# Image tiles in four quarter-row transfers; first rows of a group and stacking copies on ScalarE's queue

## What is computed

```python
def tok(x, channel_weights):                      # x: (128, 12, 224, 224)
    pooled = x.reshape(B, C, 14, 16, 14, 16).sum(axis=(3, 5))
    return jnp.einsum('bcij,ce->bije', pooled, channel_weights).reshape(B, 196, 192)
def attn(x, proj_w, proj_b):
    q, k = x[:, :64], x[:, 64:]
    a = softmax(jnp.einsum('bqc,bkc->bqk', q, k) * scale)
    out = jnp.einsum('bqk,bkc->bqc', a, k)
    out = jnp.transpose(out, (0, 2, 1)).reshape(B, -1, 192) @ proj_w.T + proj_b
    return jnp.concatenate([out, k], axis=1)
def ffn(x, ...):                                  # cw: two experts' weights of each token
    h = silu(einsum('td,eid->tei', x, w1)) * einsum('td,eid->tei', x, w3)
    return einsum('tei,edi,te->td', h, w2, cw) + shared(x)
h = tok(x); h = h + attn(layernorm(h)); h = h + ffn(layernorm(h))
```

## Time and profile before

| | us |
|---|---|
| median of 3 runs | 1790.35 |
| lowest, highest | 1789.66, 1797.8 |
| the profiled execution | 1794.41 |
| its span, first to last instruction | 1792.6 |

### The profile page before, as it was taken

One profiled execution on the slowest core, in us unless ns is written; L12 is line 12 of the kernel. 1 busy time (PEld: TensorE's weight loads), 2 busy tenths in 40 slices (PEclk: granted clock), 3 DMA queues, 4 the chain that ended last, 5 costly groups with the idle time before them and its releaser, 6 DMA issues. The chain is left out here.

```text
span 1792.6 us, 29976 instructions
## 1 busy us (share of the span) xinstructions
PE 1509.6 (84%) x9094; PEld 1184.0 (66%) x9094; DVE 1178.3 (66%) x2060; ACT 879.1 (49%) x2809; POOL 761.5 (42%) x761
## 2 busy tenths in 40 slices
PE   1721698999899988989899988999899988999997
PEld 1201575877668765877668765777668765887686
DVE  5856686687768666667768676677768666355511
ACT  2333655556545645547535655546545644335310
POOL 4327244633373234623464243633373233733431
PEclk9955799999999989999999999999999989999998
DMA  9897777778677777777777687768777775223320
GB/s 341 358 361 276 300 276 272 276 276 291 245 280 260 281 262 268 273 275 274 256 247 297 241 292 278 276 253 299 256 263 280 268 262 158 70 64 111 96 84 24
DMA packets 127672, 440.11 MB, mean 246 GB/s; under 512 B 14221, under 2 KB 80930, under 8 KB 105998
## 3 DMA queue, kind: packets, MB, share of 16 engines
q1 hardware_dynamic: 126390, 436.79, 67.6%
q10 hardware_dynamic: 1112, 1.30, 0.3%
HBM read 413.86 MB, written 20.07 MB: 242 GB/s over the span
## 5 line engine op out<-in xcount | busy, mean ns | idle before, releaser
L752 POOL TENSOR_TENSOR ffn<-ffn 128x384 f32<-128x384 f32 (+2 forms) x448 | 510.3, 1144 | 888.7 <-ACT ffn L913 810.2
L1509 PE MATMUL bank<-W2T,ffn 128*128 128x192 f32 (+1 forms) x3600 | 705.7, 333 | 10.2 <-ACT stage L890 5.0
L1509 PEld LDWEIGHTS bank<-W2T,ffn 128*128 128x128 f32 (+1 forms) x3600 | 604.9, 191 | 79.8 <-issue 16.5
L1266 DVE TENSOR_TENSOR ffn<-bank,ffn 128x384 f32<-128x384 f32 (+2 forms) x504 | 310.4, 617 | 349.3 <-PE bank L1353 151.8
L960 DVE TENSOR_REDUCE pooled<-xt 128x3 f32<-128x768 f32 (+2 forms) x375 | 447.8, 1195 | 18.5 <-DMA xt<-in_x 17.9
L913 ACT ACTIVATE ffn<-bank 128x384 f32<-128x384 f32 (+2 forms) x504 | 272.3, 542 | 370.3 <-PE bank L1524 141.3
L801 ACT ACTIVATE xt<-xt 128x256 f32<-128x256 f32 x809 | 329.7, 414 | 83.7 <-DMA xt<-in_x 76.1
L1524 PE MATMUL bank<-X2T,Wx 126*128 126x384 bf16 (+2 forms) x720 | 202.6, 355 | 46.7 <-DVE ffn L1266 31.9
L801 ACT ACTIVATION_READ_ACCUMULATOR xt<-xt 128x1 f32 x809 | 158.6, 196 | 0.0
L1353 PE MATMUL bank<-x0h,WT0h 128*128 128x512 f32 x288 | 130.5, 453 | 6.0 <-DVE ffn L1266 6.0
L1524 PEld LDWEIGHTS bank<-X2T,Wx 126*128 126x128 bf16 x720 | 58.2, 100 | 103.7 <-DVE ffn L1266 46.1
(11 more groups left out here) (234 smaller groups left out, 1786.1 us busy)
## 6 DMA issues: line engine op xcount, KB each, us to landing
xt<-in_x SPq DMA_DIRECT2D x168, 1792.0 KB, 8.2
ffn<-cw_rows SPq DMA_DIRECT2D x192, 256.0 KB, 6.8
ffn<-cw_rows SPq DMA_DIRECT2D x192, 192.0 KB, 8.8
out<-stage SPq DMA_DIRECT2D x192, 96.0 KB
ffn<-cw_rows SPq DMA_DIRECT2D x64, 224.0 KB, 7.1
h2q<-Msb SPq DMA_DIRECT2D x64, 54.0 KB
ffn<-in_L_ffn_w SPq DMA_DIRECT2D x2, 768.0 KB
attw<-in_L_ffn_w SPq DMA_DIRECT2D x1, 512.0 KB
```

The source lines that it names most:

```text
L752: nc.gpsimd.tensor_tensor(out=cwb[slot][:, 0:n], in0=silu[(g.par + step) % 2][:, 0:n], in1=cwb[slot][:, 0:n], op=ALU.mult).then_inc(scaled, 1)
L1266: v.tensor_tensor(out=h[step % HR][:, 0:n], in0=h_ps(g, step, 1)[:, 0:n], in1=(silu[p] if e == NE else cwb[(c * NE + e) % CW_RING])[:, 0:n ...
L1509: last = mm(o, h[step % HR][:, 128 * t:128 * t + m], W2T[:, e, :], start=(e == 0 and t % 2 == 0), stop=(e == NE), skip_group_check=True)
```

## The change

Each tile is read by four DMAs of a quarter of a row (128 partitions by 3584 bytes) one behind the other instead of by one; all four count on the tile's semaphore, and the sums wait for all four as before. The copies of `stack_mix` become the ACT items `mix` in steps 11 and 17, and rows 0 to 4 of the next group ACT items `row` in steps 61 and 62, each with the same DMAs, now on ACT's own queue. SP issues the rows from 5 on as before, and the tiles.

```diff
-MIX = {11: 0, 17: 1}
+AQ_PLAN[11].append(("mix", 0))
+AQ_PLAN[17].append(("mix", 1))
...
+AK_PLAN[61] = [("row", 0), ("row", 1)]
+AK_PLAN[62] = [("row", 2), ("row", 3), ("row", 4)]
...
+PIECES = 4
...
-        v = 16 * ((self.off * TILES + t) // SLOTS + 1)
+        v = 16 * PIECES * ((self.off * TILES + t) // SLOTS + 1)
...
+        def load_tile(eng, num, t, slot):
...
+            for p in range(PIECES):
+                at = slice(ROW // PIECES * p, ROW // PIECES * (p + 1))
+                eng.dma_start(xt[:, slot, at], xv[num, i, 128 * k:128 * k + 128, at]).then_inc(x_in[slot], 16)
...
-                if use == 0:
+                if use == CW_AHEAD:
                     sp.wait_ge(cw_out[0], g.at(16, 16))
...
-                if step >= 61 and left:
-                    for ahead in ((0, 1) if step == 61 else (2, 3, 4)):
-                        cw_load(g.plus(1), ahead)
-                elif step + CW_AHEAD < STEPS and g.off >= 0:
+                if step + CW_AHEAD < STEPS and g.off >= 0:
                     cw_load(g, step + CW_AHEAD)
...
-                    if step in MIX:
-                        stack_mix(g, MIX[step])
...
+                if kind == "mix":
+
+                    act.wait_ge(aux_act, g.at(BYACT[-1], BYACT[R[("M", 2 * i + 1)]]))
+                    for m in range(4):
+                        act.dma_start(Mst[:, 4 * i + m, :],
+                                      Msb[2 * CH * m:2 * CH * (m + 1), i, :]).then_inc(mixed[i], 16)
+                    return
+                if kind == "row":
+
+                    if i == 0:
+                        act.wait_ge(cw_out[0], g.at(16, 16))
+                    back = i + CW_USES - CW_RING
+                    wait(act, h_done, g.minus(1).at(STEPS, back // NE * EX + back % NE + 1) if g.k is not None or g.off else 0)
+                    if i == CW_RING - 1 or g.k is None and g.off == 0:
+                        act.wait_ge(rows_used, POOL_TILES)
+                    n = CHUNKS[0][2]
+                    act.dma_start(cwb[i][:, 0:n], cw_rows[g.par, i, 1024:1024 + n].partition_broadcast(128))\
+                       .then_inc(cw_landed[i], 16)
+                    return
```

More of the change, by code:

```diff
@@ L236, in landed @@
     def landed(self, t):
-        v = 16 * ((self.off * TILES + t) // SLOTS + 1)
-        return v if self.k is None else self.k * (16 * 2 * TILES // SLOTS) + v
+        v = 16 * PIECES * ((self.off * TILES + t) // SLOTS + 1)
+        return v if self.k is None else self.k * (16 * PIECES * 2 * TILES // SLOTS) + v
     def bank(self, r):
@@ L410, in build @@
         xv = x.rearrange("(g b) c (s i h) w -> g i (b c s) (h w)", b=GB, s=2, h=PATCH)
-        def x_rows(num, t):
+        def load_tile(eng, num, t, slot):
             k, i = t // HALF, t % HALF
-            return xv[num, i, 128 * k:128 * k + 128, :]
+            for p in range(PIECES):
+                at = slice(ROW // PIECES * p, ROW // PIECES * (p + 1))
+                eng.dma_start(xt[:, slot, at], xv[num, i, 128 * k:128 * k + 128, at]).then_inc(x_in[slot], 16)
         PREP = [("CWcT", 0), ("CWcT", 1), ("G", 0), ("gate", 0), ("repG", 0), ("gate", 1)]
@@ L487, in _ @@
             for t in range(SLOTS):
-                sp.dma_start(xt[:, t, :], x_rows(0, t)).then_inc(x_in[t], 16)
+                load_tile(sp, 0, t, t)
             sp.wait_ge(cwr_ready, 1)
@@ L505, in load @@
                 slot = g.slot(t)
-                sp.dma_start(xt[:, slot, :], x_rows(g.num(), t)).then_inc(x_in[slot], 16)
+                load_tile(sp, g.num(), t, slot)
             def store(g, c):
@@ L526, in store @@
                     sp.dma_start(dst, st[0:min(n - 128 * t, 128), t, :]).then_inc(done, 16)
[L528 to L533, removed]
             def load_after(g, t):
@@ L556, in cw_load @@
                     sp.wait_ge(cw_out[2], g.at(32, 32))
-                if use in (0, NE, QCH * NE):
+                if use in (CW_AHEAD, NE, QCH * NE):
                     sp.sem_inc(sp_passed, 1)
```

## The result

| | median us | lowest, highest | runs |
|---|---|---|---|
| before, beside it | 1793.44 | 1783.66, 1800.71 | 20 |
| after | 1803.14 | 1790.14, 1815.14 | 20 |
| ratio after/before | 1.0053 | 95%: 1.0033 to 1.0074 | |

The changed kernel is 0.5% slower, 9.5 us by the ratio. Forecast was 1789 on a median before of 1790.35 us, so the middle of "no change"; the time lies inside the range of 1768 to 1808, but the kernel moved by more than its interval. The profiled execution of after took 1797.95 us, 5 us less than its median, and is only 3.5 us longer than that of before.

A forecast was written before the change was run, and what follows sets the result against it. PE sets the pace from group 0 on, DMA engines before it. Rows -9.9, quarters +6 and +1.5, copies removed -22.3, ACT's block +17.6 and +6 sum to -1.1 us: 1789 on a median of 1790.35, range 1768 to 1808.

The forecast's parts named there:

- Rows on ACT, -9.9: Rows 0 to 4 on ACT's queue: -10.2 us at six group boundaries, -1.7 for the clock, +2 ahead of group 0.
- 3.9 + 1.5 us: Row 0's landing time after ACT's issue: 3.9 us from a small `CQ` write, 1.5 for sharing with quarter tiles.
- the 1.7 us a boundary: At the boundary of two groups, row 0 issued by ACT would land near 591.5, 1.7 us earlier than before.
- rows come no earlier: Rival: rows on ACT interleave with the tiles, and each boundary loses up to 2.3 us; late half 1803 us; chance 0.12.
- Ahead of group 0, +2 and +6: Before group 0: ACT's five row issues delay its first silu, +2 us; eighteen quarter tiles while DMA-bound, +6 (0 to 9).
- The 11%: Packets of 3.5 KB would be 11% dearer than those of 14 KB, 0.5 us on a tile's 4.6 us.
- Later quarter tiles, +1.5 (0 to 5): From group 0 on, rows issued behind a tile come 1 us later for three more issues: +1.5 us (0 to 5).
- Copies removed at `H`, -22.3: PE's 12.0 us wait for stacking copies at the first `H` goes, with 10.3 us of lower clock after it: -22.3 us.
- ACT's block, +17.6 and +6 in step 11, 0 in step 17: Four copy issues delay ACT's silu behind the step 11 exp 2.2 us a group, +17.6; clock falls +6; step 17 free.
- Signs: POOL's row waits under 40 us, PE's L1402 under 5, L1449 none for copies; exp to silu 4.6; group 0 8 later.
- block and clock at double weight: Rival: clock falls at step 14 in most groups and issues don't run beside the exp: 1806 us, chance 0.18.
- The last rival: PE's waits were another's, so the change pays prices without gains: 1797 us; counted within the forecast's chance of 0.37.

The follow-up runs named there:

- quarters_only: Kernel before with only the image tiles split into four quarter-row transfers, rows and copies staying on SP: ratio 1.0083 to before, +14.9 us.
- quarters_rows: Kernel before with quarter tiles and rows 0 to 4 issued by ACT, stacking copies staying on SP: ratio 1.0076 to before, +13.6 us.
- before_wide: Kernel before with one edit, each query chunk's four two-image stores made eight one-image stores: 1761.09 us, ratio 0.9829 to before, -30.7 us.
- after_wide: Changed kernel (all three parts) with the query chunk's four two-image stores made eight one-image stores: ratio 1.0017 to before, +3.0 us.
- quarters_wide: Kernel before with one-image stores and quarter tiles, rows and copies staying on SP: ratio 0.9891 to before, -19.5 us.
- wide_mix1: Kernel before with one-image stores and only the stacking copies of step 17 issued by ACT: ratio 0.9881 to before, -21.3 us.
- mix_only: Kernel before with only the eight stacking copies of a group issued by ACT, tiles whole, rows on SP: ratio 1.0080 to before, +14.3 us.
- wide_mix: Kernel before with one-image stores and all stacking copies issued by ACT, tiles whole: ratio 0.9954 to before, -8.2 us.
- rows_mix: Changed kernel with image tiles whole again, rows 0 to 4 and stacking copies still issued by ACT: ratio 1.0218 to before, +39.1 us.
- wide_rows: Kernel before with one-image stores and rows 0 to 4 issued by ACT, tiles whole: ratio 0.9895 to before, -18.8 us.

## Why the prediction was wrong

The sum was -1.1 us and came to +9.5. The runs give each part's worth in the order quarters, rows, copies; each of the last two is a difference of two ratios, and all are uncertain by 5 to 7 us:

| part | forecast | measured | from |
|---|---|---|---|
| quarters | +7.5 | +14.9 | quarters_only |
| rows, given quarters | -9.9 | -1.3 | quarters_rows less quarters_only |
| copies, given both | +1.3 | -4.1 | after less quarters_rows |

- **What bounds it.** Right as far as it went: PE sets the pace, and the change is worth what PE waits. But I took the late row and the late copies as a matter of which queue they stand in. The step that failed: the prediction says that SP came late to the rows "behind four stores and a tile that it got rid of slowly (1.88 us for one tile issue)" and did not ask why they were slow. before_wide shows that these stores were the cause of most of both waits: with one image in each, and rows and copies left on SP, 12.0 us became 4.1 and 10.6 became 1.7.
- **Rows on ACT, -9.9.** Landing time was the mis-sized step: 3.9 + 1.5 us against 7.7 in the boundary shown and 8.8 at the median. The neighbour that I chose, a `CQ` write of ACT's, is a small write and no row beside tiles; and rows 0 to 4 have 192 KB, not the 256 of the forecast. Counted from the silu, row 0 came 7.24 us later, before and after, so the 1.7 us a boundary were not gained. The rival "rows come no earlier" (1803, chance 0.12) described this part. That its 1803 is also the measured total is luck: it has no loss by quarters or by step 17 in it.
- **Ahead of group 0, +2 and +6.** PE waits 5.89 us there in after_wide and 4.25 with the rows back on SP, so +1.6 for the rows: right. For the quarters 6 us was too much. In quarters_only PE's first product of group 0 stands at 197.09, 0.7 us after the 196.38 of the earlier trace rows, in quarters_wide at 199.50, 3.7 us after the 195.76 of before_wide. The 11% by which quarters should have been dearer did not come: from 104 to 120 us q1 moves 6.50 MB in after at a share of 102.9%, 395 GB/s at full share against 401, so 1.5%. Nor did each tile take the 6 us more that the prediction works out from the fit of the Trainium skill without overlap; that fit, by the section "Anatomy of one DMA — SWDGE (gpsimd) path" of "DMA: Bandwidth & Descriptors", is one for DMAs that GpSimd issues, and these are SP's. The first product in quarters_only, and q1 in after from 104 to 120 us:

```profile
197.09 0.82 PE L1527 MATMUL bank<-X2T,Wx 126*128 126x384 bf16 x2 [4.24 <-ACT ffn L916]
```

```profile
q1 hardware_dynamic: 2043, 6.50, 102.9%
```

- **Later quarter tiles, +1.5 (0 to 5).** This term was too small: of 14.9 us in quarters_only at most a few lie ahead of group 0. The forecast sentence "126 more issues in each pair of groups are no matter for SP, which waits most of the time" failed. What waits behind SP's issues is not seen in an average: the copies' wait rose by 7.4 us and that at the boundary by 2.8.
- **Copies removed at `H`, -22.3.** The mechanism was right where the forecast put it. But for 0.2 us the 12.0 us stood at the first `H` of a group, and in after no first `H` waits. Groups 2 and 6 take 14.5 us each from there to L1471, at a granted clock of 1.00, where they took 18.0 and 18.4. Yet the eight stretches together are no shorter: 120.3 us against 119.4. What takes the gain is, by wide_mix1, step 17: the 6.2 us of waits at the fifth `H` and ACT's hold there. In mix_only, with whole tiles, PE's wait for `h2q<-Msb` fell to 1.2 us and the kernel was still 14.3 us slower.
- **ACT's block, +17.6 and +6 in step 11, 0 in step 17.** The total was right, 22.5 us in wide_mix against 23.6, but by luck, since it was put in the wrong place. The silu after the exp moved by 0.5 us and not by 2.2: three of the four issues started before the exp did. The 0 for step 17 failed: with its copies alone on ACT the stretches from the first `H` to L1458 take 10.9 us more (118.4 against 107.5), as much as wide_mix1 costs by its timed runs (9.4). ACT's 1.83 us of idle time there were no slack, since the issues held ACT for 2.65 us and PE lost time in every group. Through which of ACT's instructions PE loses it is not settled.
- **Signs.** POOL's waits for rows rose to 100.4 us instead of falling under 40, PE's at L1415 are 8.8 us and not under 5, and L1462 still waits. The time from the exp to the next silu grew to 2.90 us, not to 4.6; group 0 starts at 199.92 us, 3.5 later and not 8; ACT's issues took 0.4 to 0.8 us each; and the mean granted clock of the two traces is the same, 0.950.
- **Chances.** "Slower" had 0.32. The mechanism that had most of it, block and clock at double weight, was not the one. The last rival was also mis-added: its 1797 holds only the 7.5 us of the quarters, and the prices without the gains would be 1821.

What stays open: how three parts that cost 46.4 us when added up singly cost 9.5 together. The runs show that the stores of two images have the larger part in it: with one image each the parts give 45.6 by single runs and 33.7 together. How the quarters take back 29.6 us can be followed in part, from the traces of rows_mix and after, whose spans differ by 40.7 us; some 9 of them are there because one trace lies above its kernel's median and the other below. PE's waits at the boundary fall by 16.1 us (24.9 to 8.8) and those at L1471 by 7.1, those for the copies rise by 4.3, and PE's busy time falls by 18.1 (1528.9 to 1510.8 us, at a mean granted clock of 0.939 and 0.950). So shorter waits and PE's shorter busy time have about equal parts in these two traces; which wait brings on which fall of the clock is not shown.

## What to carry to other kernels

When a transfer is late, look at what stands ahead of it on its queue before moving it to another, and ask why issues of 0.3 us take 2. Here stores whose outermost size was 2 stood ahead, and one edit of their shape gave 31 us where rearranging queues lost 9.5. A queue of its own gave the rows no precedence: beside the tiles they came no earlier than from the shared queue, and one by one. Idle time of an engine is no room for issues when another engine waits for what comes behind them: four issues that should have been free in step 17 held ACT for 2.65 us and lengthened PE's work in every group. So price each place by an experiment of its own.

## What the runs showed of the hardware

- Four stores of 96 KB, two images by 64 rows, held SP for 8.98 us; eight of 48 KB, one image by 64 rows, for 5.03 us, and stores of 48 KB landed after 4.1 us at the median of the page. Four of 96 KB with 16 images outermost held it for 2.80 us. Without tiles beside them four of two images took 4.5 us.
- Rows of 192 KB on a second queue land after 12.5, 10.5, 8.8 and 7.3 us beside tiles in packets of 14336, 7168, 3584 and 2048 bytes; with the stores of one image, 8.8 us beside whole tiles (wide_rows).
- In the DMA-bound stretch of 104 to 120 us tiles in packets of 3584 bytes moved at 395 GB/s at full share (after), tiles in packets of 14336 at 401 (before).
- DMA issues of ACT started before an exp that stands ahead of them in the program: three of four started beside the silu and the table load ahead of it (from 632.30 us on, exp at 634.16).
- Parts that cost 14 to 17 us each alone cost 10 together; a part tested alone on a queue that is held up by something else says little of its own worth.
